# One language-model layer on one core: up products multiplied by the root of the routing weight and squared afterwards, VectorE's steps placed one expert further ahead, normalisation on ScalarE, all engine loops written out

## The reference

```python
h = take(table, x)
h = h + attention(layernorm(h))           # qkv, softmax over 8 positions, out projection + bias
n = layernorm(h); flat = n.reshape(-1, 256)
scores = sigmoid(flat @ Wg.T)             # 16 experts in 4 groups
topk_idx, topk_w = route(scores, bias_corr)   # 4 experts of 2 groups, w = 2.5 * s / sum(s)
cw = zeros(T, 16).at[arange(T)[:, None], topk_idx].add(topk_w)
hid = _relu2(einsum('th,eih->eti', flat, W1))
y = einsum('eti,ehi->eth', hid, W2)
out = einsum('eth,te->th', y, cw)
h = h + out + _relu2(flat @ Ws1.T) @ Ws2.T
```

## Time and profile before

| | |
|---|---|
| median of 3 executions | 1467.15 us (1464.38 to 1470.97) |
| span of the profiled execution, first to last instruction | 1464.6 us |
| mean granted TensorE clock in it | 0.961 |
| PE busy | 1267.7 us (87%) |
| DVE busy | 1189.9 us (81%) |
| ACT busy | 679.8 us (46%) |
| POOL busy | 689.5 us (47%) |
| DMA | 92.21 MB, mean 63 GB/s |

### The profile page before, as it was taken

One profiled execution on the slowest core, in us unless ns is written; L12 is line 12 of the kernel. 1 busy time (PEld: TensorE's weight loads), 2 busy tenths in 40 slices (PEclk: granted clock), 3 DMA queues, 4 the chain that ended last, 5 costly groups with the idle time before them and its releaser, 6 DMA issues.

```text
span 1464.6 us, 22940 instructions
## 1 busy us (share of the span) xinstructions
PE 1267.7 (87%) x7488; PEld 1033.1 (71%) x7488; DVE 1189.9 (81%) x1792; ACT 679.8 (46%) x1138; POOL 689.5 (47%) x753
## 2 busy tenths in 40 slices
PE   4458898889888899888989889898988989989898
PEld 2146767768677687767778677776867768677787
DVE  3868889697987969789797888969798797978854
ACT  2234444544444454444544444454553445445355
POOL 7744535365263635535464363536526363442600
PEclk9579999999999999999999999999999999999999
DMA  2302111111211112111111212112121111212122
GB/s 66 125 16 74 58 60 58 61 62 55 73 62 57 58 44 88 58 61 58 66 65 44 78 67 62 58 46 73 58 73 58 61 58 44 88 44 73 59 73 73
DMA packets 33748, 92.21 MB, mean 63 GB/s; under 512 B 4800, under 2 KB 13376, under 8 KB 33600
## 3 DMA queue, kind: packets, MB, share of 16 engines
q1 hardware_dynamic: 30528, 81.99, 16.7%
q0 software_dynamic: 3072, 8.39, 2.0%
HBM read 81.46 MB, written 8.91 MB: 62 GB/s over the span
## 4 chain that ended last, share of the span: by engine, by line
DVE 39%; PE 31%; issue 19%; POOL 5%; ACT 5%; DMA 1%; DVEq 1%; ACTq 0%; POOLq 0%; SPq 0%
PE psY L900 9%; PE psH L887 8%; DVE ring L684 7%; PE psB L927 5%; DVE p_sb L641 5%; DVE hid_lo L647 5%; PE psA L966 3%; DVE g_gt L723 2%; DVE ring L300 2%; PE psA L978 2%; DVE ring L302 2%; DVE ring L279 1%; DVE k_sb L666 1%; ACT hid_hi L510 1%; DVE stats L659 1%
## 5 line engine op out<-in xcount | busy, mean ns | idle before, releaser
L900 PE MATMUL psY<-w_hi,hid_hi 128*128 128x256 f32 x1152 | 339.0, 294 | 53.6 <-DVE hid_lo L647 50.3
L510 ACT CAST hid_hi<-p_sb 128x512 fp32r<-128x512 f32 x256 | 159.2, 622 | 388.8 <-DVE p_sb L641 379.5
L900 PE MATMUL psY<-w_lo,hid_hi 128*128 128x256 f32 x1152 | 330.5, 287 | 0.0
L900 PE MATMUL psY<-w_hi,hid_lo 128*128 128x256 f32 x1152 | 330.2, 287 | 0.0
L279 POOL TENSOR_TENSOR ring<-q_sb,k_sb 128x1024 f32<-128x1024 f32 x64 | 169.1, 2653 | 309.1 <-PE psA L940 205.2
L900 PEld LDWEIGHTS psY<-w_hi,hid_hi 128*128 128x128 f32 x1152 | 223.6, 194 | 107.4 <-DVE hid_lo L647 72.6
L647 DVE TENSOR_TENSOR hid_lo<-p_sb,hid_hi 128x512 fp32r<-128x512 f32 x256 | 214.6, 838 | 93.4 <-ACT hid_hi L510 73.7
L887 PE MATMUL psH<-xT_hi,w_hi 128*128 128x512 f32 x576 | 235.6, 409 | 10.9 <-issue 8.7
L641 DVE TENSOR_TENSOR p_sb<-r_sb,cwB 128x512 f32<-128x512 f32 x256 | 214.2, 837 | 34.1 <-ACT r_sb L499 27.2
L900 PEld LDWEIGHTS psY<-w_lo,hid_hi 128*128 128x128 f32 x1152 | 224.6, 195 | 9.8
L887 PE MATMUL psH<-xT_lo,w_hi 128*128 128x512 f32 x576 | 230.2, 400 | 0.0
(11 more groups left out here) (133 smaller groups left out, 2137.5 us busy)
## 6 DMA issues: line engine op xcount, KB each, us to landing
cwB<-cw_dram SPq DMA_DIRECT2D x128, 512.0 KB, 3.7
out<-h SPq DMA_DIRECT2D x32, 256.0 KB, 5.4
p_sb<-w_t SPq DMA_DIRECT2D x3, 512.0 KB
cwB<-w_t SPq DMA_DIRECT2D x3, 512.0 KB, 4.5
h<-w_t SPq DMA_DIRECT2D x2, 512.0 KB
xin<-table,idx_now POOLq DMA_INDIRECT x56
cwB<-wqkv_t SPq DMA_DIRECT2D x2, 384.0 KB, 3.2
cw_dram<-cwT SPq DMA_DIRECT2D x16, 32.0 KB, 1.6
```

The costliest lines, as they stand in the source:

```text
L510: nc.scalar.copy(hid[0][:, e % 2, :], src[:, e % 2, :]).then_inc(hid_hi, 1)
L900: last = nc.tensor.matmul(psY[:, j // 2, (j % 2) * D:(j % 2 + 1) * D], hid[a][:, e % 2, j * P:(j + 1) * P], W2[b][:, e, :], start=(e == 0 ...
```

## The change

It changes the following.

- An expert's routing weight is no longer multiplied in after the square. DVE's `weigh` computes max(psH, 0) x root of the weight from psH straight into r_sb, as one instruction; for the two shared experts it takes the relu alone. ACT's `square` squares r_sb twice, once into p_sb as fp32 and once into the high half; relu, the square in place and `hidden_hi` are gone. `hidden_lo` takes the difference of p_sb and the high half for all experts. psH is given free by `weigh` (semaphore r_done).
- `weigh` is called for expert e+2 after `hidden_lo(e+1)`, between the two places; it was called for e+1 at the start of e. ACT's `square(e+1)` stands at the start of e.
- POOL gets `root_weights`: three instructions on cw (128x64), a maximum with 1e-30, a power of 0.5, a product with the 0/1 mask e_gt. PE's transposition of cw waits for the third. They stand between products 1 and 3 of the next block.
- `normalise` is ACT's, four instructions of 256 columns with a scale and a bias that are both read per partition; POOL computes the bias (nmr) with one more instruction per normalisation.
- The loops of the five engines are written out for all 16 blocks, with constant thresholds; the copy of the gather's indices falls away.

```diff
-                    sp.wait_ge(p_ready, nth(blk, E, QN * (g - 1)))
+                    sp.wait_ge(r_done, nth(blk, X_ALL, SH + QN * (g - 1)) + CREDIT)
...
+            for b in range(B):
+                block_io((None, b), (None, b + 1) if b + 1 < B else None)
...
+                ts(m[:, 0, :], st[:, :, 1], -0.5, None, ALU.mult)
+                ts(m[:, 1, :], st[:, :, 4], -0.5, None, ALU.mult).then_inc(ln_step[w], 1)
...
-                tt(rstd[w][:, :], m[:, 2, :], half_neg[:, :], ALU.pow).then_inc(ln_rstd[w], 1)
+                pool.wait_ge(ln_step[w], nth(blk, 5, 4))
+                if blk[1] >= 1:
+                    pool.wait_ge(xn_ready[w], nth(blk, 1, 0))
+                tt(rstd[w][:, :], m[:, 2, :], half_neg[:, :], ALU.pow).then_inc(ln_step[w], 1)
+                pool.wait_ge(ln_step[w], nth(blk, 5, 5))
+                tt(nmr[w][:, :], m[:, 3, :], rstd[w][:, :], ALU.mult).then_inc(ln_rstd[w], 1)
+
+            def root_weights(blk):
+                pool.wait_ge(route_step, nth(blk, ROUTE_STEPS, ROUTE_STEPS))
+                nc.gpsimd.tensor_scalar(cw[:, :, :], cw[:, :, :], 1e-30, None, ALU.max).then_inc(root_step, 1)
+                pool.wait_ge(root_step, nth(blk, 3, 1))
+                nc.gpsimd.tensor_tensor(cw[:, :, :], cw[:, :, :], half[:, :, :], ALU.pow).then_inc(root_step, 1)
+                pool.wait_ge(root_step, nth(blk, 3, 2))
+                nc.gpsimd.tensor_tensor(cw[:, :, :], cw[:, :, :], e_gt[:, :, :], ALU.mult).then_inc(root_step, 1)
...
                     product(pool, nc.gpsimd, nxt, 1)
+                root_weights(blk)
+                if nxt is not None:
                     product(pool, nc.gpsimd, nxt, 3)
...
-            def relu_square(blk, e):
-                act.wait_ge(h_mm, nth(blk, X_ALL, e + 1))
-
+            def square(blk, e):
+                act.wait_ge(r_done, nth(blk, X_ALL, e + 1 + CREDIT))
                 act.wait_ge(hid_lo, nth(blk, X_ALL, e + 1))
-                nc.scalar.activation(r_sb[:, e % 2, :], psH[:, e % 2, :], ACT.Relu).then_inc(relu_done, 1)
-                act.wait_ge(relu_done, nth(blk, X_ALL, e + 1 + CREDIT))
-                nc.scalar.activation(r_sb[:, e % 2, :], r_sb[:, e % 2, :], ACT.Square).then_inc(sq_done, 1)
-
-            def hidden_hi(blk, e):
-                if e < SH:
-                    act.wait_ge(sq_done, nth(blk, X_ALL, e + 1))
-                    src = r_sb
-                else:
-                    act.wait_ge(p_ready, nth(blk, E, e - SH + 1))
-                    src = p_sb
-
+                nc.scalar.activation(p_sb[:, e % 2, :], r_sb[:, e % 2, :], ACT.Square).then_inc(sq_done, 1)
                 act.wait_ge(w2_mm, nth(blk, X_ALL, e + 1))
-                nc.scalar.copy(hid[0][:, e % 2, :], src[:, e % 2, :]).then_inc(hid_hi, 1)
+                nc.scalar.activation(hid[0][:, e % 2, :], r_sb[:, e % 2, :], ACT.Square).then_inc(hid_hi, 1)
+
+            def normalise(w, blk, src, dst):
+                act.wait_ge(ln_rstd[w], nth(blk, 1, 1))
+                d = dst[:, :, :].rearrange("p a t -> p (a t)").rearrange("p (j d) -> p j d", d=D)
+                for j in range(TT):
+                    last = nc.scalar.activation(d[:, j, :], src[:, j, :], ACT.Identity,
+                                                bias=nmr[w][:, j:j + 1], scale=rstd[w][:, j:j + 1])
+                last.then_inc(xn_ready[w], 1)
...
+                if h == V_NORM2:
+                    normalise(1, blk, h1[blk[1] % 2], v_sb)
...
+                if h == V_NORM1:
+                    normalise(0, blk, xin[blk[1] % 2], k_sb)
...
                 for e in range(X_ALL):
                     if e + 1 < X_ALL:
-                        relu_square(blk, e + 1)
+                        square(blk, e + 1)
                     elif att is not None:
-                        relu_square(att, 0)
-                    for h, last in ((2 * e, False), (2 * e + 1, True)):
+                        square(att, 0)
+                    for h in (2 * e, 2 * e + 1):
                         if att is not None:
                             attention(att, h)
                         if nxt is not None:
                             head(nxt, h)
-                        if last:
-                            break
-                        if e + 1 < X_ALL:
-                            hidden_hi(blk, e + 1)
-                        elif att is not None:
-                            hidden_hi(att, 0)
...
             def weigh(blk, e):
 
+                dve.wait_ge(h_mm, nth(blk, X_ALL, e + 1))
+                dve.wait_ge(hid_hi, nth(blk, X_ALL, e + 1))
                 if e < SH:
+                    nc.vector.tensor_scalar_max(r_sb[:, e % 2, :], psH[:, e % 2, :], 0.0).then_inc(r_done, 1)
                     return
                 r = e - SH
-                dve.wait_ge(sq_done, nth(blk, X_ALL, e + 1))
                 if r % QN == 0:
                     g = r // QN
                     dve.wait_ge(cwB_in[g % 2], nth(blk, 16 * QS // 2, 16 * (g // 2 + 1)))
-
-                dve.wait_ge(hid_hi, nth(blk, X_ALL, e + 1))
-                nc.vector.tensor_tensor(p_sb[:, e % 2, :], r_sb[:, e % 2, :],
-                                        cwB[:, (r // QN) % 2, r % QN, :], ALU.mult).then_inc(p_ready, 1)
+                nc.vector.scalar_tensor_tensor(r_sb[:, e % 2, :], psH[:, e % 2, :], 0.0, cwB[:, (r // QN) % 2, r % QN, :],
+                                               ALU.max, ALU.mult).then_inc(r_done, 1)
 
             def hidden_lo(blk, e):
-                src = r_sb if e < SH else p_sb
+                dve.wait_ge(sq_done, nth(blk, X_ALL, e + 1))
                 dve.wait_ge(hid_hi, nth(blk, X_ALL, e + 1 + CREDIT))
-                nc.vector.tensor_tensor(hid[1][:, e % 2, :], src[:, e % 2, :],
+                nc.vector.tensor_tensor(hid[1][:, e % 2, :], p_sb[:, e % 2, :],
                                         hid[0][:, e % 2, :].bitcast(f32), ALU.subtract).then_inc(hid_lo, 1)
...
             def block_dve(blk, att, nxt):
                 for e in range(X_ALL):
-                    if e + 1 < X_ALL:
-                        weigh(blk, e + 1)
                     for h, last in ((2 * e, False), (2 * e + 1, True)):
                         if att is not None:
                             attention(att, h)
@@ -845,6 +812,10 @@
                             hidden_lo(blk, e + 1)
                         elif att is not None:
                             hidden_lo(att, 0)
+                        if e + 2 < X_ALL:
+                            weigh(blk, e + 2)
+                        elif att is not None:
+                            weigh(att, e + 2 - X_ALL)
                 add_experts(blk)
 
             for h in range(V_T1):
...
-                pe.wait_ge(relu_done, nth(blk, X_ALL, e + 1))
+                pe.wait_ge(r_done, nth(blk, X_ALL, e + 1))
...
-                pe.wait_ge(route_step, nth(blk, ROUTE_STEPS, ROUTE_STEPS))
+                pe.wait_ge(root_step, nth(blk, 3, 3))
```

More of the change, by code:

```diff
@@ L122, in lm_tower_layer @@
         rstd = [sb(f"rstd{w}", [P, TT]) for w in range(2)]
+        nmr = [sb(f"nmr{w}", [P, TT]) for w in range(2)]
+        half = sb("half", [P, TT, E])
         lg = sb("lg", [P, TT, 2, E])
@@ L609, in _ @@
                 head((None, 1), h)
[L610 to L617 removed]
+            square((None, 0), 0)
+            for b in range(B):
+                block_act((None, b), (None, b + 1) if b + 1 < B else None, (None, b + 2) if b + 2 < B else None)
         @block.vector
@@ L622, in _ @@
             dve.sem_inc(hid_lo, CREDIT)
+            dve.sem_inc(r_done, CREDIT)
             dve.sem_inc(y_added, 1)
@@ L864, in _ @@
                 head((None, 1), h)
+                if h == LOGITS + 3:
+                    weigh((None, 0), 0)
+                    weigh((None, 0), 1)
             hidden_lo((None, 0), 0)
-            with dve.Fori(0, B // 2 - 1) as i:
-                block_dve((i, 0), (i, 1), (i, 2))
-                block_dve((i, 1), (i, 2), (i, 3))
-            block_dve((None, B - 2), (None, B - 1), None)
-            block_dve((None, B - 1), None, None)
+            for b in range(B):
+                block_dve((None, b), (None, b + 1) if b + 1 < B else None, (None, b + 2) if b + 2 < B else None)
         @block.tensor
@@ L1046, in _ @@
                     up((None, 0), 1)
-            with pe.Fori(0, B // 2 - 1) as i:
-                block_pe((i, 0), (i, 1), (i, 2))
-                block_pe((i, 1), (i, 2), (i, 3))
-            block_pe((None, B - 2), (None, B - 1), None)
-            block_pe((None, B - 1), None, None)
+            for b in range(B):
+                block_pe((None, b), (None, b + 1) if b + 1 < B else None, (None, b + 2) if b + 2 < B else None)
 def kernel(x, L0_tok_weight, L0_attn_qkv_proj, L0_attn_qkv_bias, L0_attn_out_proj, L0_attn_out_bias,
```

78 lines of the change are left out of this document (18 added, 60 removed).

## The result

The changed kernel takes **1698.5 us** (1697.24 to 1699.92, 4 executions) where the kernel before took 1469.06 on the same chip: ratio 1.156 [1.153, 1.160]. It is slower by 229 us; the forecast was 1444, its range ended at 1510.

A forecast was written before the change was run, and what follows sets the result against it. VectorE was taken to bound each block before the out projection, TensorE after it. Per block -3.3 + 1.2 + 1.5 = -0.6, 15 blocks -9, loops -16, first and last block +2: -23, so 1444 us, range 1400 to 1510.

The forecast's parts named there:

- TensorE waits 1.2 + p: At the transposition of cw, with p the power's time: TensorE waits this instead of 1.7 us, p - 0.5 a block.
- so at few columns start-up rules; I take the end near that: GpSimd's power on 64 columns, judged from its flat additions: 2.0 us, between readings of 1.2 and 13.6.
- The rival of the dear power: GpSimd's power costs per column with TensorE standing behind it: slower, 1489 us at 5 us, 1618 at 13.6; chance 0.27.
- Stretch A: Block's first 52.39 us, up to the out projection, bound by VectorE: -3.3 us a block, between -1.5 and -6.
- B: The 33.90 us from the out projection on, bound by TensorE; VectorE has 10 us free there.
- without scatter: VectorE's `weigh`, reading PSUM, no longer waits behind GpSimd and takes 0.69 us: gain 0.5 a block, at most 2.4.
- shrink because the high half is now ready an expert ahead: VectorE's 1.9 us of waits for ScalarE before the out projection shrink: gain 1.4 us a block.
- The softmax: One `weigh` that covered ScalarE's exponential now stands ahead of it, and VectorE waits: loss of 0.7 us a block.
- The block's start: One low half stays short, but expert 2's `weigh` waits for cwB: net gain 1.3 us a block, between 0 and 2.6.
- The second: Normalisation before TensorE's second transposition, longer on ScalarE with GpSimd's added product: +1.2 us a block, between 0 and 2.
- The first: Normalisation of 1.38 us leaving VectorE, counted half because what follows waits for TensorE: gain 0.8 a block, at most 1.4.
- The loops: -16: Blocks where a loop turns are 2.2 us longer; writing out removes 7 turns: -16 us, between 0 and -18.

The follow-up runs named there:

- with the product: The changed kernel with a product by the same constant tile in place of GpSimd's power (weight halved, not rooted): 1529.4 us.
- the late order: The changed kernel without root, normalisations on VectorE, squares between the places, weigh for e+1 at the start of e: 1440.8 us.
- the order alone: The changed kernel without the root and with both normalisations back on VectorE, leaving written-out loops and the new order of weigh and square: 1528.4 us.
- the repaired order: Kernel before with loops written out, weigh(e+1) at start of e, squares between the places, normalisations on VectorE, root in ScalarE's copy: 1441.2 us.

## Why the prediction was wrong, step by step

**The root: the mechanism was right, the price was not.** "TensorE waits 1.2 + p": with p = 10.74 that is 11.9, and 14 of the 16 waits were 11.92; with the product, p = 0.47, it is 1.7, and 14 were 1.65. The maximum took 1.28 us beside VectorE's product, as said, and 0.81 in the last block, where only a low half of 0.69 ran there. The step that failed is "so at few columns start-up rules; I take the end near that", p = 2.0. It took a power for an addition with more start-up, though the row gave two readings and its rival had the other one: "if all of it is per column, 0.21 x 64 + 0.2 = 13.6". The runs give 0.156 a column. The estimate came from the flatness of another operation, which says nothing of this one. The rival of the dear power, with a chance of 0.27, was right in place and kind; by its sum p = 10.7 is +108 us. (The prediction puts the end of its range at p about 6.7; by the same sum 1510 us is p = 6.4.) The Trainium skill, "GPSIMD Engine Reference", section 3.1, gives about 2.6 cycles for an element of an ordinary two-input operation, 0.13 us as an estimate for 60 more columns. The product is near it (0.20 us on 4 columns, 0.29 on 64); for the power the same columns took 9.35 us more.

**Stretch A: forecast -3.3 us a block, of which -2.5 for the order of weigh and square; that order measured +5.2** (whole block, 85.15 to 90.32 us, with the loops alone as base). By medians over blocks 2 to 12, A goes from 51.6 to 55.2 us and B from 33.6 to 35.3, so a third of the loss lies in B, where the prediction expected none. By parts:

- `weigh` takes 0.683 us without scatter, from 0.837: right, some 2.5 us of work a block; with the late order, where nothing else loses, it is worth nothing that can be told (1440.8 against 1442.9 us).
- The waits for ScalarE "shrink because the high half is now ready an expert ahead": this, a gain of 1.4 a block, is the step that failed. ScalarE's square now waited for VectorE, and the attention's high halves stood behind it in ScalarE's list: a loss of 41 us, 2.6 a block. The prediction asked only whether ScalarE's own work matters (it is 46% busy), never what is queued behind the new wait.
- The softmax: "a loss of 0.7". The wait of 0.70 us was there (10.5 us in 15 waits). The loss at experts 3 and 4 is 2.1 to 2.4 us a block with the early weigh there (1.0 in the changed kernel, behind its stall). The weigh of 0.6 and the wait, both on the chain through maximum, exponential and spread, explain 1.3; the rest was not taken apart.
- The residual at place 23, in stretch B: not named at all, and worth 25 us.
- The block's start: the wait for cwB was foreseen with sign and size (some 2 us after VectorE is ready; 37.1 us in 13 waits with the order alone, 19.7 in 16 in the changed kernel), but the net gain of 1.3 is not seen: experts 0 to 2 take 12.3 us in the new order and 12.1 with the loops alone.

**The normalisations: sign and size were about right.** The second was put at +1.2 a block, between 0 and 2. It costs 11 us by difference in the old order, and expert 12 is 0.7 us longer with it in the new one (8.17 to 8.88). Its four instructions take 2.08 us, where 2.4 was counted. TensorE's wait there is 1.74 us in the changed kernel; the order alone already makes it 1.0 (16.1 us in 16 waits). The first was put at -0.8, at most -1.4: between the order alone and the change without the root, which differ in both normalisations, expert 5 gets 1.3 us shorter (5.12 to 3.84), and the whole of both is 1526.5 against 1528.4 us. So neither explains the slowdown. In the old order, though, the first costs 29 us, for the same reason as the squares: it took work off VectorE and stood ahead of something urgent on ScalarE.

**The loops: -16, measured -26.** The sign and the equal periods were right (11 of the 15 distances from block to block are 85.14 to 85.16); the short blocks were taken as free of the turn and were not.

**Together.** Forecast: power +22, A -50, second normalisation +18, loops -16, first and last block +2. Measured: power 169 to 172, order and both normalisations together +84, loops -26, which makes 1468.6 + 230. Had p alone been right, the forecast would have been 1444 + 15 x 8.74 = 1575, still 123 too low.

## What to carry to other kernels

An engine that works in order carries the waits of its whole list: before an instruction gets a new releaser or a new place, write down what stands behind it on that engine and who waits for that, and do it for idle engines above all. The order of weigh and square cost 85 us while the busy time of VectorE fell from 1183 to 1171 us, ScalarE's from 678 to 505 and GpSimd's from 693 to 654. And an operation whose cost is known at one size only has two readings, a start or a price per element; where nothing in the trace tells them apart and nothing hides the instruction, the dear one has to be priced as the likelier outcome, or the operation put where it is hidden: the same root in ScalarE's copy cost nothing in the repaired order.

## What the runs showed of the hardware that was not expected

- A power on GpSimd costs 0.156 us a column over 128 partitions, 10.51 to 10.76 us for 64, with both sets of values tried; a product of 64 takes 0.29 to 0.49.
- VectorE's instructions with two SBUF operands took 0.68 to 0.69 us beside a power of GpSimd, and up to 2.9 beside a product of 1024 columns.
- 31 loads of ScalarE's tables (1.28 us each) cost the kernel 21.5 us in one order and nothing that can be told in another (1441.2 against 1440.8).
- After a stall of 12 us TensorE was granted 0.53 of its clock over the next 3 us; after the 1.65 us of the version with the product it was granted 1.00 over as long a stretch.
